# Edge positions found in half columns, and the edge scatters begun in the first stage

## The reference

```python
sums = jax.ops.segment_sum(edge_attr, src, num_segments=n)       # graph branch
counts = jax.ops.segment_sum(jnp.ones(...), src, num_segments=n)
edge_attr_agg = sums / jnp.maximum(counts, 1.0)[:, None]
h = relu(concat([x, edge_attr_agg, u[batch]]) @ W1 + b1); gnn = h @ W2 + b2
...
for i in range(4):                                               # mixer branch
    h = layernorm(x) * ln1_g[i] + ln1_b[i]
    q = softmax(h @ Wq, per head); k = softmax(h @ Wk, over all nodes)
    x = x + (q @ (k^T @ (h @ Wv))) @ Wo + bo
    h = layernorm(x) * ln2_g[i] + ln2_b[i]
    x = x + gelu(h @ W1[i] + b1[i]) @ W2[i] + b2[i]
...
x = x + gnn + mixer
idx = argmax(layernorm(x) @ router_w.T + router_b)               # one of 32 experts
x = x + relu(relu(z @ W1[idx] + b1[idx]) @ W2[idx] + b2[idx])
```

## Time and profile before

| what | us |
|---|---|
| three runs | 2933.5, 2939.52, 2940.58 |
| median | 2939.52 |
| profiled execution, span from first to last instruction | 2931.4 |
| median less that span (launch and end, not in the profile) | 8.1 |
| first stage and its drain, within the span | 76 to 315 |
| pass 0, from ACT's first high half to its last | 316.9 to 778.7 |
| pass 1, the same | 836.2 to 1296.4 |
| pass 2, the same | 1355.0 to 1837.5 |

### The profile page before, as it was taken

The page is one execution under the profiler, slowest core; times in us unless marked ns, Lnnn a source line. Parts: engine busy times, 40 slices in busy tenths (PEclk is TensorE's granted clock), DMA queues, the critical chain, the costliest instruction groups (busy, mean ns, idle before and its releaser), DMA issues.

```text
span 2931.4 us, 57571 instructions
## 1 busy us (share of the span) xinstructions
PE 2633.3 (90%) x19546; PEld 2460.0 (84%) x19546; DVE 2140.1 (73%) x4842; ACT 1577.9 (54%) x3079; POOL 1771.3 (60%) x1613
## 2 busy tenths in 40 slices
PE   4888899999999999998899999789999998996298
PEld 2767899999988999998899999789999898995265
DVE  8887677777767777776667777688888887896064
ACT  0554466666636666663566666344444445673075
POOL 2011188888768888876888888355555554222666
PEclk7998999999999999999999999899999998997599
DMA  6001222223232322223223232243333322210243
GB/s 125 28 30 35 81 62 65 67 61 70 56 97 66 67 69 63 65 55 103 68 60 68 63 68 54 58 120 88 89 89 87 90 80 63 62 37 23 81 129 97
DMA packets 255567, 207.98 MB, mean 71 GB/s; under 512 B 165505, under 2 KB 194386, under 8 KB 255277
## 3 DMA queue, kind: packets, MB, share of 16 engines
q1 hardware_dynamic: 197678, 162.55, 21.1%
q0 software_dynamic: 57600, 41.75, 7.2%
HBM read 136.93 MB, written 70.16 MB: 71 GB/s over the span
## 4 chain that ended last, share of the span: by engine, by line
PE 40%; POOL 25%; DVE 15%; issue 13%; DMA 2%; ACT 2%; DVEq 1%; SPq 1%; another core or an unknown queue 0%; POOLq 0%; ACTq 0%
PE bank L390 36%; POOL edges_sorted L765 19%; PE bank L1870 3%; DVE hidh_lo L1352 3%; POOL r L743 2%; POOL tokens_sorted L830 2%; DMA staging<-in_edge_attr 2%; DVE xh L1316 2%; DVE oh L1548 1%; DVE staging L1222 1%; POOL ehl L782 1%; DVEq L1527 1%; PE bank L2333 1%; DVE bn L1307 1%; DVE kmask L1216 1%
## 5 line engine op out<-in xcount | busy, mean ns | idle before, releaser
L765 POOL DMA_INDIRECT edges_sorted<-staging,pos_i x850 | 1079.5, 1270 | 251.5 <-issue 233.0
L881 ACT ACTIVATE hid<-bank,b1p 128x250 f32<-128x250 f32 x800 | 331.5, 466 | 324.3 <-PE bank L390 274.0
L390 PE MATMUL bank<-w_hi,hidh_hi 128*125 128x256 f32 x1600 | 471.3, 295 | 23.5 <-DVE hidh_lo L1352 23.5
L390 PE MATMUL bank<-h_hi,w_hi 128*128 128x250 f32 x1600 | 479.9, 300 | 9.2 <-DVE h_lo L1336 8.9
L390 PE MATMUL bank<-w_hi,hidh_lo 128*125 128x256 f32 x1600 | 453.0, 283 | 0.0
L390 PE MATMUL bank<-w_lo,hidh_hi 128*125 128x256 f32 x1600 | 451.2, 282 | 0.0
L390 PE MATMUL bank<-h_hi,w_lo 128*128 128x250 f32 x1600 | 448.6, 280 | 0.0
L390 PE MATMUL bank<-h_lo,w_hi 128*128 128x250 f32 x1600 | 445.2, 278 | 0.0
L1352 DVE TENSOR_TENSOR hidh_lo<-hid,hidh_hi 128x500 fp32r<-128x500 f32 x400 | 320.4, 802 | 164.7 <-ACT hidh_hi L887 118.5
L390 PEld LDWEIGHTS bank<-w_hi,hidh_hi 128*125 128x125 f32 x1600 | 299.5, 187 | 32.0 <-DVE hidh_lo L1352 28.8
L390 PEld LDWEIGHTS bank<-h_hi,w_hi 128*128 128x128 f32 x1600 | 304.2, 190 | 16.2 <-DVE h_lo L1336 11.4
(11 more groups left out here) (294 smaller groups left out, 6648.4 us busy)
## 6 DMA issues: line engine op xcount, KB each, us to landing
staging<-edges_sorted SPq DMA_DIRECT2D x103, 260.0 KB
staging<-in_edge_attr SPq DMA_DIRECT2D x50, 531.2 KB
queries<-qn SPq DMA_DIRECT2D x100, 250.0 KB
qin<-queries SPq DMA_DIRECT2D x100, 250.0 KB
edges_sorted<-staging,pos_i POOLq DMA_INDIRECT x850
rows_in<-edges_sorted SPq DMA_DIRECT2D x50, 260.0 KB
yin<-tokens_sorted SPq DMA_DIRECT2D x81, 127.0 KB
raw<-in_L_mix_W SPq DMA_DIRECT2D x8, 1024.0 KB, 5.5
```

What stands on the lines that cost most here:

```text
L390: return nc.tensor.matmul(o, left, right, start=start, stop=stop, skip_group_check=True)
L765: nc.gpsimd.indirect_dma_start(out=edges_sorted, out_offset=bass.IndirectOffsetOnAxis(ap=pos_i[:, i:i + 1], axis=0), in_=stage[:, slot, j, ...
L881: a = nc.scalar.activation(hid[c % 2][:, j, :], chunks(PH[c % 2])[:, j, :], ACT.Gelu, bias=b1p[:, 2 * c + j:2 * c + j + 1])
```

## The change

Positions are worked out in units of half a column: 100 units, first the 50 kinds of columns 0 to 425, then those of columns 426 to 849. Each unit has its own mask of half a column (8 slots for 4), its own two products and its own placing, and a unit's placing waits for the one before it. 16 units are early, then four per step for t = 0 to 20. `pos_i` is cast in two parts, at t = 8 and t = 21; `pos_f` moves from slot 0 of `staging` to `scr[2]`, whose place `w1` takes later, hence two new waits on `pos_ready`.

The first two attribute loads move from step (0, -1) to step (-1, 9). Scatters begin with step (-1, 10), three behind `key_sum` in each of 15 steps (45), then 31 in drain(-1) behind its last `key_sum`, and in passes 0 to 2 five ahead of the root and five behind it in every step from t = -1 on (10 for 11 or 12). By the ends of drains -1, 0 and 1 that makes 76, 350 and 624, and 850 at t = 21 of pass 2. SP handles the drain's first span of scatters within the drain, ahead of `load_down`.

```diff
-SCATTERS_DRAIN = 14
-SCATTERS_STEP = {0: (5, 6), 1: (5, 6), 2: (5, 7), 3: (4, 4)}
+CUT = HALF + 1
+RANK_PARTS = (slice(0, CUT), slice(CUT, ECOL))
+UNITS = 2 * TILES
+SLOTS = 2 * MASKS
-RANKS_EARLY = 8
+RANKS_EARLY = 16
-PLACED_AT = 22
+PLACED_AT = (8, 21)
+SCATTERS_DRAIN = {-1: (6, 25), 0: (14, 0), 1: (14, 0)}
+SCATTERS_STEP = {-1: (0, 3), 0: (5, 5), 1: (5, 5), 2: (5, 5), 3: (4, 4)}
+SCATTERS_FROM = PLACED_AT[0] + 2
...
-        pos_f = stage[:, 0, :, :].rearrange("p c r -> p (c r)")[:, 0:ECOL]
+        pos_f = scr[2]
...
-            for l in range(LAYERS):
-                for t in range(-1, GROUPS):
-                    if t >= (2 if l == 0 else 0):
-                        plan[l, t] = SCATTERS_STEP[l]
-                plan[l, GROUPS] = (SCATTERS_DRAIN, 0) if l < LAYERS - 1 else (EDGES, 0)
+            for l in range(-1, LAYERS):
+                for t in range(SCATTERS_FROM if l < 0 else -1, GROUPS):
+                    plan[l, t] = SCATTERS_STEP[l]
+                plan[l, GROUPS] = SCATTERS_DRAIN.get(l, (EDGES, 0))
...
+        def placed(c):
+            return 1 if (c + 1) * CH <= CUT else 2
...
             def load_attr(c):
                 slot = c % 2
-                sp.wait_ge(pos_ready, 1)
+                sp.wait_ge(pos_ready, placed(c))
...
             def step(l, t):
                 if 0 <= l and t + 3 < GROUPS:
                     load_queries(l, t + 3)
-                if l == 0 and t == -1:
+                if l == -1 and t == SCATTERS_FROM - 1:
                     load_attr(0)
                     load_attr(1)
                 if l >= 0 and t == -1:
-                    attr_after(l - 1, GROUPS)
+                    attr_after(l - 1, GROUPS, slice(1, None))
...
                 store_queries(l + 1, LAST - 1)
+                attr_after(l, GROUPS, slice(0, 1))
                 load_down(l + 1)
...
-            def kind_place(b):
-                for h in range(2):
-                    part = slice(h * HALF, (h + 1) * HALF)
-                    dve.wait_ge(e_rank, KINDS + 2 * b + h + 1)
-                    nc.vector.copy_predicated(pos_f[:, part], kmask[(KINDS + b) % MASKS][:, part].bitcast(U16),
-                                              PH[h][0:P, 0:HALF]).then_inc(e_acc, 1)
+            def kind_mask(u):
+                b, part, _, mask = rank_unit(u)
+                if u >= SLOTS:
+                    dve.wait_ge(e_acc, u - SLOTS + 1)
+                else:
+                    dve.wait_ge(e_rank, KINDS - MASKS + u // 2 + 1)
+                nc.vector.tensor_scalar(mask, kind16[:, part], float(b), None, ALU.is_equal).then_inc(e_mask, 1)
+
+            def kind_place(u):
+                _, part, width, mask = rank_unit(u)
+                dve.wait_ge(e_rank, KINDS + u + 1)
+                if u:
+                    dve.wait_ge(e_acc, u)
+                nc.vector.copy_predicated(pos_f[:, part], mask.bitcast(U16), PH[u % 2][0:P, 0:width]).then_inc(e_acc, 1)
```

More of the change, by code:

```diff
@@ L1272, in _ @@
             stepped()
-            for i in range(KINDS + MASKS):
-                kind_mask(i)
+            for k in range(KINDS):
+                count_mask(k)
+            for u in range(SLOTS):
+                kind_mask(u)
             first_ranks()
@@ L1278, in early_ranks @@
             def early_ranks(first, end):
-                for b in range(first, end):
-                    kind_place(b)
-                    kind_mask(KINDS + MASKS + b)
+                for u in range(first, end):
+                    kind_place(u)
+                    kind_mask(SLOTS + u)
             for t in range(TILES):
@@ L2201, in _ @@
             edge_starts()
-            for b in range(RANKS_EARLY):
-                rank_edges(b)
+            for u in range(RANKS_EARLY):
+                rank_edges(u)
             pe.wait_ge(rows_loaded, 7 * 16)
```

72 lines of the change are left out of this document (41 added, 31 removed).

## The result

The changed kernel takes 2950.56 us (median of 12 runs, 2946.04 to 2956.49) where the kernel before, run beside it, takes 2939.59 (12 runs, 2933.5 to 2950.1). The ratio is 1.0038, 95% interval 1.0027 to 1.005: slower by 11 us, 8 to 15. The forecast was 2975 with a range of 2952 to 3000. The sign was right and the size was not.

What follows compares the result with a forecast made beforehand. It took DVE to bound the first stage, POOL the passes' early steps and nearly all of pass 2, PE pass 1's late part. Terms 9.5 + 2 + 8 + 41 + 11 - 36 gave +35.5, so 2975 us, range 2952 to 3000.

Steps and rivals of the forecast that it cites:

- Term 1: First stage, on DVE: more and smaller masks and more placings lengthen it by 9.5 us.
- Term 2: First stage: scatters on POOL hold up masks on DVE, +2 us, 0 to 15.
- Term 3: Step 9, first stage: attribute loads after T (cast ending step 8) delay a query store; DVE waits, +8 us, 4 to 13.
- term 6: Early and late parts of passes: ten scatters a step leave PE the bound, -36 us, -26 to -42.
- Term 4: Ahead of the first root: 36 scatters on POOL delay that root, +41 us, 38 to 44.
- Term 5: Pass starts: PE's lower clock, a later second root and later mixer weights, +11 us, 4 to 15.
- Rival B: SP's queue: held issues delay three more first-stage stores, mixer weights come later, 2998 us; chance 0.14.
- A2: All passes: PE follows POOL, so all 69 steps fall towards 16.9 us, time 2818 us; chance 0.04.
- faster: Whole kernel: the measurement shows it faster than before, beyond about 0.3% (9 us); chance 0.06.
- some other gain: Whole kernel: a gain from a cause not named, no size given; chance 0.04.

Runs made afterwards that it cites:

- e2: Changed kernel with (6, 10) scatters in drain(-1) for (6, 25), so 21 ahead of the first root for 36: 2902.61 us, 0.995 of the kernel before.
- e1: Changed kernel with no scatters in drain(-1), the five of step (0, -1) kept: 2887.58 us, 0.9897 of the kernel before.
- e7: e5 with two scatters for five behind each pass's first root, seven between first and second root for ten: 2870.74 us, 0.9831 of the kernel before.
- e8: e5 with nine scatters (5, 4) for ten in the first six steps of each pass: 2881.04 us, 0.986 of the kernel before.
- e3: Changed kernel's half-column units and early cast alone, scatters and attribute loads as in the kernel before: 2926.56 us, 1.0031 of the kernel before.
- e6: Changed kernel with the drain's attribute load back behind W2's load in passes 1 and 2: 2960.54 us, 1.0115 of the kernel before.
- second pair: Profiles of the kernel before and the changed kernel, both unchanged, repeated on one other chip: 2925.37 and 2938.66 us.
- e4: Kernel before with only scatters moved (five in drain(-1), ten a step early, eleven later) and first two attribute loads in drain(-1): 2903.68 us, 0.9959 of it.
- e5: e4 with the attribute load freed by a drain's scatters issued inside the drain, ahead of W2's load: 2894.37 us, 0.9897 of the kernel before.

## Why the prediction was wrong in size

The path was right: the burst ahead of the first root is the largest cost, the early and late parts are the gain. The step that failed is the first stage, terms 1 to 3: 19.5 us were carried to its end, and 6.7 arrived. Term 3 took a hold of SP's queue for a wait of DVE that never came (8 us for none), and terms 1 and 2 carried 11.5 us through. Beside that term 6 was put 3.5 to 7.2 us too small, and the drains, put at nothing, gave 2 to 4.

**Term 4, +41: right.** 38.9 and 40.5. I offered 38 for the bare price of 1.49 us and took 1.566; e2 shows 1.49 in such a burst. The room of 15.68 us was used up as said, and e1 and e2 show that nothing of the rest is given back. The first root came at 360.26 for the 374 of the forecast, and 12.8 of these 13.7 us are terms 1 to 3.

**Term 6, -36: right, a little small.** -43 and -39.5. Early parts of 109 and a late part of 332 were forecast and measured to 2.3 us. But POOL's period did not fall to 16.9: with no idle time ahead of a root it is the length of an early step, 17.8 to 18.2 us, so at ten scatters POOL is as full there as PE. And PE's busy time of 106.5 us was no floor: in the earlier trace rows it is 107.15 at a clock of 1.00, where e7's products take 104.87 at the same clock, so some of it is not work, and elsewhere some of it is the lower clock. "Fewer than ten would bring nothing" is refuted by e8's early parts, though by little: at full clock 104.50 for e7's 105.13.

**Term 3, +8: did not occur.** The step that failed carried the durations of the earlier trace rows to another place. SP there had W2's load of 1 MB just ahead of the two attribute loads, and the second of them took 11.34 us to issue. In step (-1, 9) SP had nothing large ahead, and the second took 5.66. SP in the changed kernel's first stage, and DVE's waits for the stores of queries from 76 to 280 us:

```profile
140.81 6.03 SPq L619 DMA_DIRECT2D staging<-in_edge_attr  x2
148.01 4.84 SPq L606 DMA_DIRECT2D queries<-qn  x1
```

```profile
DVE qn L1508 <- DMA queries<-qn: 0.6, 1, 0.6
```

With T at 140.81, the store behind the loads was issued by T + 12.0 for the T + 18 of the forecast. It was held for 4.84 us itself. DVE's next write of `qn` came at 157.59, T + 16.8 for the T + 12.5 forecast: the step was taken at 8.3 us, and this one takes 10.30 (10.29 in e3, which has no loads there). So the store had 4.8 us in which to land, and DVE did not wait. e3 confirms it: without these loads in that stage its end comes no earlier. The sign that the prediction named, a wait of some 8 us around 150 us, is missing.

**Term 1, +9.5: 7.4 to 7.9 in e3, 6.7 in the changed kernel.** The masks and placings by form, 84 to 257 us:

```profile
L1248 DVE COPY_PREDICATED scr<-kmask,bank 125x424 f32<-125x424 uint16 x50 | 31.5, 629 | 0.4
L1241 DVE TENSOR_SCALAR kmask<-kind 125x424 bf16<-125x424 bf16 x50 | 20.1, 401 | 1.7
```

Placings of 629 ns for an estimate of 630, and masks of 275 ns (those of 426 columns, where no scatter runs) for 0.28. In the steps ahead of POOL's sums that gives the 0.22 a kind of the forecast: e3's take 6.94 us for 6.50. Beside POOL's sums it does not. The step of 7.85 us takes 7.97 in e3, 0.06 a kind: of the two half masks one waits for the sum and takes 0.70 us, where the whole mask took up to 1.15. The 8.24 to 8.28 us of the changed kernel hold another 0.3 us of scatters beside masks, so that its period met the 8.3 of the forecast is luck. (The lower end of the term, +6, is not what its own numbers give; with masks of 0.195 they give about 2.5.) The sums of exponentials slipped 8.2 us by 264 us into the span, but only 6.7 at the last of them. In the drain DVE is not the bound (the last sums wait 4.1 us for ACT), and some of the lag is given back there. I carried all of it through.

**Term 2, +2: nothing on the path**, 1.7 us of DVE's time (above). The Trainium skill ("SBUF — State Buffer", section "Who interferes with whom") says that a two-port DVE instruction and a GpSimd instruction exclude each other for a whole instruction; for scatters this trace disagrees. A scatter on POOL and a mask on DVE that begins and ends within it:

```profile
158.33 1.18 POOL L783 DMA_INDIRECT edges_sorted<-staging,pos_i  x1 [0.30 <-issue]
...
158.85 0.27 DVE L1241 TENSOR_SCALAR kmask<-kind 125x424 bf16<-125x424 bf16 x1
```

From 150 to 257 us five masks lie like this and take what they take alone. The six of 0.54 to 0.59 us began 0.67 us or more into a scatter and ended 0.07 us behind it, so only the later part of a scatter holds a mask up. Beside POOL's sums the trace agrees: in e3 each of the seven masks of this stretch that began while a sum ran took some 0.70 us and ended 0.13 us behind it.

**Term 5, +11: near in sum (9.7, 9.0), wrong in parts.** The second root's 16.7 us behind the first became 18.14 in pass 0 and 16.9 to 17.3 in the others, and that is the whole cost: e7, with it at 12.74, is back at starts of 14.6 us in passes 1 and 2. I gave it nothing of its own. The mixer weights that I charged with 3 us a pass came earlier: ACT's waits of 6.1, 2.2 and 2.0 us for them fell to 1.1, 1.1 and none. The clock behind PE's long wait (1.2 GHz until shortly behind the first high half; 0.60 from 363 to 369 us) cost 0.5 us up to that high half, for 2; what more it cost lies ahead of the second, where PE had to wait for the root in any case (2.1 us of it left).

**What was left out.** The drains of the passes gave 2 to 4 us. And the load that goes ahead of W2's was in the diff, and I read past it. It kept the change from losing another 22 us (e6). Rival B was right that SP's queue is the danger, but had it at the wrong place and with the wrong victim: POOL, not a store or the weights.

**The base.** I added 8.1 us for launch and end to the span. The profiled run was the fastest of the three (2933.5), so these are 2 us, and the other 6 are spread between runs. No difference rests on it. Of the chances, "faster" at 0.06 is below the 0.08 that A2 and "some other gain" have together.

In numbers (first pair): 35.5 forecast; less 12.8 (terms 1 to 3), 2.1 (term 4), 1.3 (term 5), 7.2 (term 6) and 4.2 (drains) is 7.9. In the second pair the same five are 12.7, 0.5, 2.0, 3.5 and 2.4, which leaves 14.4. The medians, 11 and 12, lie between. Nearly half of the miss is the first stage, where I added up three costs of which two met slack (the store's, DVE's in the drain).

## What to carry over

Work that fills an engine's idle time is free up to the length of that idle time and full price past it: count the room (15.68 us here; ten scatters in it moved the root by about 1 us in e4 and e5) before counting the gain that it buys elsewhere. When moved work crosses a buffer's end at another place, look up where the load that refills the buffer stands in its queue, since a consumer that waits in order passes the wait on to whatever stands behind it. How long an issue is held depends on what stands ahead of it in the queue, so a duration read at one place does not hold at another. And an engine's busy time is a floor only where its clock is full and nothing in it is waiting.

## What was not expected of the hardware

A wait of PE of 2.1 to 3.5 us at a pass's start was followed by a few us at 1.2 GHz at 23 of 24 places, and waits of 0.7 to 1.4 us at none of three (e7). PE then shows no idle time and is slow: 34 products in 6 us for 49. With three scatters fewer behind the first root, e7 has the short waits and no fall there, and is 4.5 us a pass faster.

What is issued on SP right behind an attribute load is held: 5.66 us (the second load at 141.18), 4.84 (a store, 148.01), 5.87, 5.56 (a weight load at 369.42 of the changed kernel). With W2's load ahead as well it was 11.34. A load issued alone takes 0.28 (848.90). A merged row of two issues can also hold a semaphore's wait, as the 12.81 us at 825.75 do, and only the queue's own waits tell them apart.

The time of the kernel before differs by up to 23 us between chips (2939.6 and 2916.6), and the stores of `nodes_out` took 127.5 to 152.1 us in the profiles. Either difference is more than the change itself is worth. Only pairs run together could show it.
